# A transformer block's attention in blocks of two units, with transposes and shared steps in three PSUM banks in turn

## What is computed

```python
mod = (silu(c) @ wmod).reshape(32, 6, 1, -1)          # sa, ca, ga, sb, cb, gb
h = layernorm(x) * (1 + ca) + sa
q, k, v = ...                                          # h @ Wq, h @ Wkv: 16 heads of 64
s = einsum('bhid,bhjd->bhij', q * 64 ** -0.5, k)       # 256 x 256 for each head
p = where(above_diagonal, 0, exp(s - max(s)))
out = (p @ v) / (sum(p) + 1e-8)
x = x + ga * (out @ Wo + bo)
h = layernorm(x) * (1 + cb) + sb
hq = fp4(h); gate, up = hq @ fp4(w_gate).T, hq @ fp4(w_up).T      # 352 wide
x = x + gb * (fp4(silu(gate) * up) @ fp4(w_down).T)
```

## Time and profile before

| | us |
|---|---|
| median of three runs | 1408.5 |
| the profiled execution's own time | 1407.76 |
| its span, first to last instruction | 1405.9 |
| one iteration in the middle of the span | 41.94 |
| TensorE busy | 1333.2 |
| ScalarE busy | 998.4 |
| VectorE busy | 974.4 |
| GpSimd busy | 846.4 |

### The profile page before, as it was taken

How to read it: one execution, slowest core, us unless ns; L and a number is a source line. 1 busy time by engine, 2 the same in 40 slices (tenths; PEclk the granted TensorE clock), 3 DMA queues, 4 the chain that set the end, 5 groups by cost and what they waited for, 6 DMA issues and landing times.

```text
span 1405.9 us, 34736 instructions
## 1 busy us (share of the span) xinstructions
PE 1333.2 (95%) x10194; PEld 1008.6 (72%) x10194; DVE 974.4 (69%) x2405; ACT 998.4 (71%) x3301; POOL 846.4 (60%) x1582
## 2 busy tenths in 40 slices
PE   5999999999999999999999999999999999999974
PEld 3677777777777777777777777777777777777753
DVE  5557776677776677767677767677777677777664
ACT  3877777777777777767777777777777777777750
POOL 1556556666656666655666655666655666655653
PEclk7999999999999999999999999999999999999995
DMA  3000000000000000000000000000000000000000
GB/s 97 16 18 16 11 21 21 17 21 16 12 16 21 17 21 19 15 11 21 17 21 21 15 9 21 17 21 21 15 9 21 17 21 21 15 9 17 17 18 10
DMA packets 38057, 26.54 MB, mean 19 GB/s; under 512 B 2800, under 2 KB 33392, under 8 KB 38032
## 3 DMA queue, kind: packets, MB, share of 16 engines
q1 hardware_dynamic: 38032, 26.23, 6.4%
HBM read 21.94 MB, written 4.28 MB: 19 GB/s over the span
## 4 chain that ended last, share of the span: by engine, by line
PE 72%; issue 9%; DVE 9%; ACT 8%; POOL 1%; DMA 1%; ACTq 0%; SPq 0%; DVEq 0%; POOLq 0%
PE ps_m L796 18%; PE ps_s L883 17%; PE ps_t L775 13%; PE ps_m L833 8%; PE ps_o L906 7%; DVE probs_t L765 4%; PE ps_s L892 4%; ACT probs L546 4%; PE ps_m L857 3%; PE ps_m L775 2%; DVE neg_max L753 2%; ACT h_r L528 1%; DVE den_eps L759 1%; ACT probs_t L556 1%; ACT hq_t L523 1%
## 5 line engine op out<-in xcount | busy, mean ns | idle before, releaser
L546 ACT ACTIVATE probs<-ps_s,neg_max 128x128 f32<-128x128 f32 (+1 forms) x1024 | 424.1, 430 | 77.5 <-PE ps_s L892 77.5
L753 DVE TENSOR_REDUCE neg_max<-ps_s 128x4 f32<-128x1024 f32 x256 | 311.6, 1217 | 77.0 <-PE ps_s L883 69.9
L426 POOL TENSOR_SCALAR probs<-probs,r_den 128x256 f32<-128x256 f32 (+1 forms) x768 | 350.1, 471 | 0.0
L775 PE MATMUL ps_t<-ident,probs 128*128 128x128 f32 x1536 | 274.1, 287 | 31.8 <-DVE probs_t L765 15.6
L883 PE MATMUL ps_s<-qk 64*128 64x256 f32 x2048 | 291.5, 403 | 0.0
L424 POOL TENSOR_TENSOR probs<-probs,r_den 128x128 f32<-128x128 f32 x256 | 107.8, 421 | 299.8 <-DVE r_den L762 290.4
L775 PEld LDWEIGHTS ps_t<-ident,probs 128*128 128x128 f32 x1536 | 158.8, 140 | 114.9 <-issue 86.9
L514 ACT COPY qk<-ps_m 128x512 f32<-128x512 f32 x256 | 152.4, 595 | 112.5 <-PE ps_m L796 112.5
L906 PE MATMUL ps_o<-probs_t,v 128*64 128x256 f32 (+1 forms) x2048 | 223.0, 339 | 1.1 <-ACT o_t L537 0.7
L546 ACT ACTIVATION_READ_ACCUMULATOR probs<-ps_s,neg_max 128x1 f32 x1024 | 219.6, 214 | 0.0
L883 PEld LDWEIGHTS ps_s<-qk 64*128 64x128 f32 x2048 | 176.9, 186 | 54.6 <-issue 27.3
(11 more groups left out here) (108 smaller groups left out, 1898.3 us busy)
## 6 DMA issues: line engine op xcount, KB each, us to landing
mod_a<-mod_rows SPq DMA_DIRECT2D x32, 256.0 KB, 3.3
x_in<-L_attn_x SPq DMA_DIRECT2D x32, 128.0 KB, 2.1
x_res<-L_attn_x SPq DMA_DIRECT2D x32, 128.0 KB, 2.1
out<-y_out SPq DMA_DIRECT2D x32, 128.0 KB, 1.8
mod_b<-mod_rows SPq DMA_DIRECT2D x32, 64.0 KB, 2.8
wkv<-L_attn_Wkv SPq DMA_DIRECT2D x2, 512.0 KB, 7.0
wq<-L_attn_Wq SPq DMA_DIRECT2D x1, 512.0 KB, 4.0
wo<-L_attn_Wo SPq DMA_DIRECT2D x1, 512.0 KB, 8.4
```

What stands on the lines that cost most here:

```text
L426: ins = nc.gpsimd.tensor_scalar(cols, cols, r_den[:, par, s:s + 1], 1.0, ALU.mult, ALU.mult)
L546: ins = nc.scalar.activation(probs[:, u % 4, h, t * P:(1 + 2 * t) * P], ps_s[:, 2 * par + h, t * N:t * N + (1 + t) * P], ACT.Exp, bias=neg ...
L753: nc.vector.tensor_reduce(neg_max[:, par, :], ps_s[:, 2 * par:2 * par + 2, :].rearrange("p b (t j) -> p (b t) j", t=2), AX.X, ALU.max, neg ...
L775: return nc.tensor.transpose(dst, src, ident[0:n, 0:n])
```

## The change

An iteration has four **blocks** j = 0 to 3 of two units each (`PAIRS`). On PE a block is: scores of units 2j and 2j+1 (four heads), the values of the pair of units two blocks before (four heads, into the full width of `ps_o`), the two masks of unit 2j, places 0 and 1, the two masks of unit 2j+1, places 2 to 8. The probability transposes become shared steps of kind "t": the twelve of a pair are three groups of four at places 0, 2 and 5, one block later than their exponentials. `ps_t` is gone and `ps_m` has three banks, so that places 0, 3, 6 share a bank, 1, 4, 7 another, and 2, 5, 8 the third. Groups 0 and 1 are copied out by DVE and group 2 by ACT, 512 columns at a time. `out_copy` copies 512 columns for a pair. The other shared steps get new places, and the order on DVE, ACT, POOL and SP is written anew by blocks. The rounding of xq on POOL moves from the end of an iteration to block 0 of the next. The small tiles neg_max, den, den_eps and r_den get four slots in place of two.

```diff
-        neg_max = sb("neg_max", [P, 2, 4])
-        den = sb("den", [P, 2, 4])
-        den_eps = sb("den_eps", [P, 2, 4])
...
+        den_eps = sb("den_eps", [P, 4, 4])
+        r_den = sb("r_den", [P, 4, 4])
         probs = sb("probs", [P, 4, 2, 3 * P])
-        probs_t = sb("probs_t", [P, 2, 2, 3 * P])
...
-        ps_t = ctx.enter_context(nc.psum_tensor("ps_t", [P, 512], F32))
         ps_o = ctx.enter_context(nc.psum_tensor("ps_o", [P, 512], F32))
-        ps_m = [ctx.enter_context(nc.psum_tensor(f"ps_m{n}", [P, 512], F32)) for n in range(2)]
+        ps_m = [ctx.enter_context(nc.psum_tensor(f"ps_m{n}", [P, 512], F32)) for n in range(3)]
...
+        PLACES = {
+            (0, 3): ("xqt", 2, 0), (0, 4): ("v", 0, 0), (0, 7): ("gate", 2, 0), (0, 8): ("up", 2, 0),
+            (1, 3): ("wo", 1, 0), (1, 4): ("gate", 2, 1), (1, 7): ("v", 0, 1), (1, 8): ("up", 2, 1),
+            (2, 3): ("wo", 1, 1), (2, 4): ("v", 0, 2), (2, 7): ("v", 0, 3), (2, 8): ("xt", -1, 0),
+            (3, 3): ("hqt", 2, 0), (3, 4): ("hqt", 2, 1), (3, 7): ("down", 2, 0), (3, 8): ("down", 2, 1)}
+        for j in range(PAIRS):
+            for g, n in enumerate((0, 2, 5)):
+                PLACES[j, n] = ("t", 0, 3 * (j - 1) + g) if j > 0 else ("t", 1, 3 * (PAIRS - 1) + g)
+            for k, n in enumerate((1, 6)):
+                PLACES[j, n] = ("qk", 0, 2 * (j + 1) + k) if j < PAIRS - 1 else ("qk", -1, k)
...
+        def bank_read(kind, b, part):
+
+            if kind == "t":
+                return pt_ready[part % 3], PAIRS * b + part // 3 + 1
+            ready, per_batch = READ[kind]
+            return ready, per_batch * b + (part + 1) * per_batch // PARTS[kind]
+
+        T_ON_ACT = (2,)
...
+                for j in range(PAIRS):
+                    if has.unit(2 * j - 1):
+                        normalize(i, 2 * j - 1)
+                    if j == 0 and has.prev2:
+                        pool.wait_ge(xq_steps, QUANT_STEPS * (i - 1))
...
+                            pool.wait_ge(xqt_full, i - 2)
+                        quantize_round(nc.gpsimd, Steps(pool, xq_round, ROUND_STEPS, i - 2), xq, 2 * P // BLOCK, scale[0],
+                                       qy[0], qm[0])
+                    if j == 1 and has.prev:
...
+                    if j == 1 and has.next:
                         rstd(i + 1, ln1_pool, ln1_steps, LN_STEPS * (i + 2), mv1, var1, rstd1)
-                    if u == 5 and has.prev:
-                        rstd(i - 1, ln2_pool, x1_steps, X1_STEPS * i, mv2, var2, rstd2)
...
+                    if j in (2, 3) and has.prev2:
+                        round_hidden(i - 2, j - 2)
+                    if j == 3 and has.prev:
...
-                    if u == 7 and has.prev:
-                        pool.wait_ge(xq_steps, QUANT_STEPS * i)
-                        if has.prev2:
-                            pool.wait_ge(xqt_full, i - 1)
-                        quantize_round(nc.gpsimd, Steps(pool, xq_round, ROUND_STEPS, i - 1), xq, 2 * P // BLOCK, scale[0],
-                                       qy[0], qm[0])
...
+                    if has.attn:
+                        normalize(i, 2 * j)
+                    if j == 0 and has.prev2:
+
+                        if not isinstance(i, int) or i > 2:
+                            pool.wait_ge(y_ready, 2 * (i - 2))
+                        pool.wait_ge(wo_scaled, 2 * (i - 1))
+                        nc.gpsimd.tensor_tensor(x1_keep[:, :, :], attn[:, :, :], x_gb[:, :, :], ALU.add).then_inc(kept, 1)
+                    if j == 2 and has.prev:
+                        rstd(i - 1, ln2_pool, x1_steps, X1_STEPS * i, mv2, var2, rstd2)
...
                     def out_copy():
-                        act.wait_ge(o_full, UNITS * i + (u - 3) + 1)
-                        nc.scalar.copy(o_t[:, (u - 3) % UNITS, :], ps_o[:, 0:N]).then_inc(ot_ready, 1)
...
+                        if j == 2 and has.prev:
+                            act.wait_ge(wo_full, 2 * i)
+                        at = 2 * ((j - 2) % PAIRS)
+                        act.wait_ge(o_full, PAIRS * i + j - 1)
+                        nc.scalar.copy(o_t[:, at:at + 2, :], ps_o[:, :].rearrange("p (u j) -> p u j", u=2)).then_inc(ot_ready, 1)
+
+                    def exponentials(u, h):
                         act.wait_ge(masked, 16 * i + 2 * u + h + 1)
+                        if h == 0 and has.after(u - 4):
+                            act.wait_ge(pt_full, 3 * PAIRS * i + 3 * (u // 2 - 1))
...
+                    has_out = has.unit(2 * (j - 2))
+                    if has.attn:
+                        exponentials(2 * j, 0)
+                        exponentials(2 * j, 1)
+                    if has_out and j == 1:
                         out_copy()
-                    if has.unit(u - 2) and u in PT0_ON_ACT:
-                        act.wait_ge(pt_full, 16 * i + 2 * (u - 2) + 1)
-                        nc.scalar.copy(probs_t[:, u % 2, 0, :], ps_t[:, 0:3 * P]).then_inc(pt0_ready, 1)
-                    shared_reads(u, "a")
-                    if has.unit(u - 2):
-                        act.wait_ge(pt_full, 16 * i + 2 * (u - 2) + 2)
-                        nc.scalar.copy(probs_t[:, u % 2, 1, :], ps_t[:, 0:3 * P]).then_inc(pt1_ready, 1)
-                    shared_reads(u, "b")
+                    for n in (0, 1, 2, 3):
+                        shared_reads(n)
                     if has.attn:
-                        exponentials(0)
-                    shared_reads(u, "c")
-                    if has.unit(u - 3) and u in OT_LATE:
-                        if has.prev:
-                            act.wait_ge(wo_full, 2 * i)
+                        exponentials(2 * j + 1, 0)
+                    shared_reads(4)
+                    shared_reads(5)
+                    if has.attn:
+                        exponentials(2 * j + 1, 1)
+                    for n in (6, 7, 8):
+                        shared_reads(n)
+                    if has_out and j != 1:
                         out_copy()
...
+                def shared_reads(j, n):
+                    kind, b, k, bank, _ = shared.get((j, n), (None, 0, 0, 0, None))
+                    if kind == "t" and k % 3 not in T_ON_ACT:
+                        dve.wait_ge(pt_full, 3 * PAIRS * b + k + 1)
+                        nc.vector.tensor_copy(probs_t[:, 4 * (k % 3):4 * (k % 3) + 4, :],
+                                              ps_m[bank][:, :].rearrange("p (c j) -> p c j", c=4)).then_inc(pt_ready[k % 3], 1)
...
+                for j in range(PAIRS):
+                    if has.unit(2 * j - 1):
+                        denominators(2 * j - 1)
+                    if has.attn:
+                        maxima(2 * j)
+                    if j == 3 and has.next:
+
+                        dve.wait_ge(ht_ready, 2 * (i + 2))
+                        nc.vector.tensor_tensor(h_r[1][:, :], h_t[:, :], h_r[0][:, :], ALU.subtract).then_inc(hr_ready, 1)
+                    if has.attn:
+                        maxima(2 * j + 1)
+                    shared_reads(j, 0)
+                    shared_reads(j, 2)
+                    if has.attn:
+                        denominators(2 * j)
+                    if j in (1, 2) and has.prev2:
+                        hidden_scales(i - 2, j - 1)
+                    if j == 3 and has.prev:
+                        dve.wait_ge(ln2_pool, 2 * i)
+                        normalized([xn2[:, t * P:t * P + P] for t in range(2)], x1, mv2, rstd2, xn2_ready)
+                    shared_reads(j, 3)
+                    if j == 0 and has.next:
                         dve.wait_ge(x_loaded, 16 * (i + 2))
                         layer_norm_stats(x_in, stats1, mv1, ln1_steps, LN_STEPS * (i + 1))
-                    if u in (2, 4) and has.prev2:
-                        hidden_magic(i - 2, u // 2 - 1)
-                    if u in (1, 3) and has.prev2:
-                        hidden_scales(i - 2, u // 2)
-                    if u == 2 and has.next:
+                    if j == 1 and has.next:
                         dve.wait_ge(ln1_pool, 2 * (i + 2))
                         normalized([xn[:, t, :] for t in range(2)], x_in, mv1, rstd1, xn_ready)
-                    if u == 4 and has.prev:
+                    shared_reads(j, 4)
+                    shared_reads(j, 5)
+                    if j in (1, 2) and has.prev2:
+                        hidden_magic(i - 2, j - 1)
+                    if j == 2 and has.prev:
                         dve.wait_ge(x1_steps, X1_STEPS * (i - 1) + 2)
                         layer_norm_stats(x1, stats2, mv2, x1_steps, X1_STEPS * (i - 1) + 2)
...
+                    shared_reads(j, 7)
+                    shared_reads(j, 8)
+                    if j == 3 and has.prev:
                         dve.wait_ge(h2_ready, i)
...
                         quantize_magic(nc, Steps(dve, xq_steps, QUANT_STEPS, i - 1, SCALE_STEPS), h2, 2 * P // BLOCK,
                                        inverse[0], qy[0], qm[0])
...
```

(68 more changed lines are left out.)

159 lines of the change are left out of this document (47 added, 112 removed), and 4 rows, old and new, of the table PLACES.

## The result

The kernel after the change takes 1419.7 us (median of four runs, 1418.1 to 1420.8), the kernel before 1408.2 on the same chip. The ratio is 1.0082, with an interval of 1.0065 to 1.0100: 0.8% slower. The forecast was 1401.

The account below looks back on a forecast made before the run. TensorE, 95% busy, was taken as the bound: 38.0 us of work plus 3.55 of stalls give 41.6 to 41.7 an iteration against 41.94. Gaining 0.25 in each of 30 iterations (7.5 us) gives 1401, range 1350 to 1445.

Parts of the forecast that it names:

- the one from block 3 into block 0: VectorE's down reading and xq work precede block 0's denominators and maximum: first unit's masks at 4.5, not 3.4, 1.15 lost.
- xqt: Block 0: POOL normalizes unit 7, then rounds xq until 7.15; PE wants xqt at 6.6, 0.65 lost.
- the end: End of the kernel: loses about 2 us, as xq's scales now stand behind down.
- The forecast's 38.0: PE's work in one iteration after the change, without stalls: 38.0 us, 3.9 less than before.
- wo: Block 1: ACT copies values only after the first unit's exponentials, so wo starts at 6.0, not 5.5; 0.55 lost.
- values of block 3: Block 3: the values bank holds PE from 1.9 to 2.35, 0.4 lost.
- v in block 1: Place 7 of block 1 shares gate's bank, so v starts at 9.85 instead of 9.55, 0.3 lost.
- VectorE's busy time: DVE's load in an iteration, rising from 29.8 to 33.6 us through eight copies of 512 columns.
- A, stalls hidden: Rival: engines run earlier than forecast, half of the 3.6 us of stalls goes, 1347, down to 1290; chance 0.17.
- B, the first norm beside POOL: Rival, block 1: first norm meets POOL's work, costing 2.05 instead of 0.7; v stalls 1.65, 1441; chance 0.33.
- C, the loss at the second unit's scores and values too: Rival: scores behind another unit's scores drain all the same, 1.4 an iteration, 1443; chance 0.05.
- a margin of 0.25 us an iteration: Gain forecast for each of 30 iterations: 41.6 to 41.7 against 41.94 us, 7.5 us in all.

Follow-up runs that it names:

- the control: The kernel before with VectorE's loop turning once for two iterations: 1408.9 us, ratio 1.0006.
- the cleared path: The kernel after with ScalarE copying group 1, xq's scales and magic before down's reading, xq's rounding before unit 7's normalization: 1404.9 us, ratio 0.9979.
- the best version: The kernel after with the cleared path's three edits, values copied out early in blocks 1 and 2, VectorE's loop turning once for two iterations: 1360.1 us, ratio 0.9663.

## Why the prediction was wrong

**The step that failed is the one from block 3 into block 0.** "DVE is free at 2.9, denominators 0.3, maximum 1.22, wait 0.14: masks A at 4.5." VectorE was free at 2.92. It then stood for 0.54 at the loop's turn, which the sum does not have, and the masks started at 5.06. xqt came late by the same half microsecond, 7.86 after the block's start against 7.25 in the sum. The forecast said of this very stretch that "before, this work had a whole unit of cover"; it did not ask what else had been under that cover. The iteration was forecast at 41.67 and is 42.10: 0.43 off, and the turn is 0.54. Removing half of the turns gave back 0.31 an iteration, and the control showed that the turn had cost nothing before. Over 28 iterations this is 12 us of the 21 by which the profiled execution (1420.8 against 1400) missed its forecast.

**The term that was mis-sized is the end**, put at +2 and measured at +9.0, 7 us more of the 21. The cause was named rightly (xq's scales stand behind down), but in the last iterations nothing comes between: VectorE waits 4 us for down, and POOL and TensorE behind it. This is 3.5 of the 9.0 for the last batch; 5.8 more were lost over the iteration before it, where xq and the probabilities behind it came late in the same way and the clock was lower. Moving the scales alone gave back 2.4 of it, the cleared path 7.9.

**What held.** The forecast's 38.0 takes a block's second unit at 0.86 for the scores and 0.64 for the values, with nothing lost to a change of shape between two units. That was an estimate, and no row of the kernel before shows it; in the kernel after the scores of both units take 1.92 to 1.93 against its 1.92, and both values 1.45 against 1.44. Work of TensorE: 42.1 less the four waits of 3.3 leaves 38.8, against 38.0 and 0.8 of small stalls in the forecast. The stalls: masks 1.66 late against 1.15, xqt 0.75 against 0.65, wo 0.45 against 0.55, values of block 3 0.45 against 0.4; v in block 1 did not wait until the copies came early, then 0.34 against 0.3. A copy of 512 columns by VectorE is 0.689 against 0.68. VectorE's busy time was put too high, 33.6 against 30.8. The copies cost what was forecast (123 us more over the span), but the same sum left the rest as it was, and there the first norm took 41 us less and `den_eps` 19 less. In this kernel nothing hangs on it: taking a group away from VectorE changed nothing.

**The rivals.** *A, stalls hidden*: refuted, all four stand near or above the size forecast. *B, the first norm beside POOL*: refuted, VectorE in order of time has

```profile
705.81 0.61 DVE L705 SCALAR_TENSOR_TENSOR xn<-x_in,mv,rstd 128x128 f32<-128x128 f32 x2
```

against 2.05 in the earlier trace rows. *C, the loss at the second unit's scores and values too* (its 1.4 an iteration is 0.20 and 0.16 in each of four blocks): refuted, 0.86 for the second unit's scores and 1.45 for both values.

The sign hung on a margin of 0.25 us an iteration. The forecast's own terms give more: 38.0 and 3.55 are 41.55, 0.39 under 41.94, and it took 41.6 to 41.7. With either margin, a single missed wait of half a microsecond was enough to turn it. The stalls were real and could be moved, and with them moved the change is worth 3.4%.

What stays open: how the 0.54 of a turn is made up and when it shows (0.23 behind `y_out`, none where `y_out` ran beside POOL's rounding), and why the masks still wait 1.0 in the best version; no experiment took these apart.

## What to carry to other kernels

When a change removes the wait in front of the first instruction of a loop's body, price the loop's turn on that engine (here 0.54 us, and 2.4 with four iterations in a pass): it was paid all along, under that wait. In a queue in strict order it counted here where an instruction stands, more than how full the queue is, so find for each new wait the instruction in front that nobody is waiting for, and move that; the moves have to be tried together, since three that brought nothing singly brought 1%, and one that was worth nothing alone was worth 49 us among the others. Forecast the last iteration by itself: what the steady state hides there stands bare.

## What was not expected of the hardware

**A loop's turn.** 0.54 us between the last instruction of VectorE's body and the first of the next pass, against 0.13 between the same two within a pass, without any transfer of instructions in the loop. It is no fixed price: with `y_out` last in the body it is 0.23, and with `y_out` 0.57 to 0.58 long beside POOL's rounding (0.30 in the kernel after) there is no idle time left. With four iterations in the body a turn takes some 2.4, with 37 packets on the queue of instructions between 210 and 1260 us against none in the kernel after.

**The clock after a wait.** With group 1 given back to VectorE, the masks of unit 0 wait 1.9 us in most iterations and 2.4 in eight. In seven places between 150 and 1300 us the granted clock fell after it. Windows of this kernel around one of them, and TensorE in order of time at the same step of that iteration and of the next:

```profile
728.00:731.00 3.00, 1.08 (x13) 0.80 (x9) 2.93 (x7) 0.25 (x1) 2.76 (x6) 1.00 0.19 60
731.00:732.00 1.00, 1.00 (x10) 0.87 (x9) 1.00 (x2) 1.00 (x7) 0.23 (x1) 0.84 0.17 44
732.00:735.00 3.00, 3.00 (x13) 2.60 (x12) 1.65 (x6) 1.76 (x9) 0.65 (x2) 0.50 0.02 6
```
```profile
730.34 0.39 PE L925 MATMUL ps_s<-later_b,ident_b 128*128 128x256 bf16 x2 [1.92 <-DVE neg_max L733]
...
733.33 1.63 PE L821 MATMUL ps_m<-wkv_r,h_r 128*128 128x512 f32 x3
...
772.74 0.39 PE L925 MATMUL ps_s<-later_b,ident_b 128*128 128x256 bf16 x2 [1.91 <-DVE neg_max L733]
...
775.39 0.95 PE L821 MATMUL ps_m<-wkv_r,h_r 128*128 128x512 f32 x3 [0.22 <-ACT qk L526]
```

The clock fell after five waits of 1.9 and two of 2.4; after the other waits of either length it was full. After an idle time of 1.92 the granted clock is at 0.50 in the window from 732 to 735, and v takes 1.63 in place of 0.95; after 1.91 in the next iteration it stays full. By windows of 1 us, what the seven falls take from the granted clock is 11.9 us in all. With four iterations in a pass there are six, 13.6 us, one at each of six turns, where the masks wait 3.4 to 3.5. In the kernel after, where the same wait is 1.61 to 1.64, there is none between 150 and 1300 us, nor in the kernel before or in the best version.

**VectorE beside GpSimd.** In the kernel with four iterations in a pass, beside POOL's rounding (791.95 to 792.68), VectorE's `y_out` takes 0.68:

```profile
792.15 0.68 DVE L703 TENSOR_TENSOR y_out<-ffn,x_keep 128x128 f32<-128x128 f32 x1
```

With POOL idle it is 0.29 (at 727.23 in the kernel before), and beside POOL's normalization in the kernel after 0.30 to 0.52. The `y_out` above ends 0.15 after POOL's instruction, and the next one, 0.57 long from 793.06, ends 0.14 after POOL's next (792.76 to 793.49). Why VectorE takes longer there no run shows. It was not in the forecast, and it is a small price of moving xq's rounding to where down is read.
